# Attention and a top-1 mixture of experts on one core: the first expert tiles placed ahead of the last group's routing, the last expert's weights loaded in another order and place

## The reference

```python
x = x + attention(layernorm(x), ctx, ctx)     # per token: 16 x 16 scores over heads of width 16, causal over heads
xf = layernorm(x).reshape(4096, 256)
top1 = argmax(xf @ gate_w.T + gate_b)         # E = 8 experts
for e in range(8):                            # w1: 1024 x 256, w2: 256 x 1024
    y = relu(xf @ w1[e].T + b1[e]) @ w2[e].T + b2[e]
    out = out + where(top1 == e, y, 0)
x = x + out
```

## Time and profile before

| | us |
|---|---|
| runs | 484.26, 487.8, 488.61 (median 487.8) |
| profiled execution: its time | 486.96 |
| its span | 485.2 |
| PE busy | 397.5 (82%) |
| DVE busy | 348.3 (72%) |
| POOL busy | 206.3 (43%) |
| ACT busy | 179.6 (37%) |

### The profile page before, as it was taken

How to read it: one execution, slowest core, us unless ns; L and a number is a source line. 1 busy time by engine, 2 the same in 40 slices (tenths; PEclk the granted TensorE clock), 3 DMA queues, 4 the chain that set the end, 5 groups by cost and what they waited for, 6 DMA issues and landing times.

```text
span 485.2 us, 16314 instructions
## 1 busy us (share of the span) xinstructions
PE 397.5 (82%) x5967; PEld 337.0 (69%) x5967; DVE 348.3 (72%) x777; ACT 179.6 (37%) x317; POOL 206.3 (43%) x213
## 2 busy tenths in 40 slices
PE   0134868896887967987859999999999999999992
PEld 0024767796787866977847887777788878887871
DVE  7987879689965965777547886787666667666662
ACT  3333255552633332332323433334334333333420
POOL 8336375234574456623711342465332233232221
PEclk9999999999999755565559999999999999999998
DMA  8999668899786665676621423465333222222300
GB/s 287 415 296 237 139 149 238 213 269 261 172 212 141 157 134 125 161 162 124 218 61 33 79 83 123 132 192 179 70 71 76 77 64 64 70 63 67 85 24 0
DMA packets 105162, 69.39 MB, mean 143 GB/s; under 512 B 78077, under 2 KB 88190, under 8 KB 104576
## 3 DMA queue, kind: packets, MB, share of 16 engines
q1 hardware_dynamic: 75696, 56.67, 43.9%
q10 hardware_dynamic: 25984, 3.21, 4.8%
q0 software_dynamic: 3408, 8.46, 4.7%
HBM read 48.28 MB, written 12.57 MB: 125 GB/s over the span
## 4 chain that ended last, share of the span: by engine, by line
PE 58%; DMA 10%; POOL 7%; SPq 7%; issue 7%; DVE 6%; ACT 2%; ACTq 1%; POOLq 0%; DVEq 0%
PE s_ps L1216 22%; PE at_ps L1231 7%; DMA arena<-qv_hl 7%; PE pv_ps L1231 7%; SPq L298 7%; PE pv_ps L1130 5%; PE at_ps L1232 4%; PE pv_ps L1232 3%; PE s_ps L1098 3%; POOL sorted_rows L1037 2%; PE tr_ps L1143 2%; PE st_ps L1183 2%; DMA arena<-x 2%; POOL qv_hl L990 1%; PE lg_ps L1158 1%
## 5 line engine op out<-in xcount | busy, mean ns | idle before, releaser
L1216 PEld LDWEIGHTS s_ps<-arena 128*128 x1872 | 131.5, 99 | 44.3 <-issue 5.8
L1216 PE MATMUL s_ps<-arena 128*128 128x128 f16 x1872 | 156.8, 221 | 2.4 <-issue 2.3
L903 DVE SCALAR_TENSOR_TENSOR arena<-arena,s_ps 128x512 f32<-128x512 f32 x78 | 53.6, 687 | 43.6 <-PE s_ps L1216 43.5
L1063 POOL DMA_INDIRECT result<-arena x39 | 38.8, 995 | 79.1 <-DVE arena L927 76.6
L1098 PEld LDWEIGHTS s_ps<-k_hl,arena 128*128 128x128 f16 x1536 | 53.9, 118 | 26.1 <-DMA arena<-qv_hl 21.7
L1098 PE MATMUL s_ps<-k_hl,arena 128*128 128x16 f16 x1536 | 54.1, 181 | 19.6 <-DMA arena<-qv_hl 19.0
L1130 PE MATMUL pv_ps<-a_hl,arena 128*128 128x16 f16 x1536 | 53.9, 181 | 18.2 <-DMA arena<-qv_hl 14.0
L1130 PEld LDWEIGHTS pv_ps<-a_hl,arena 128*128 128x128 f16 x1536 | 52.7, 118 | 21.5 <-DMA arena<-qv_hl 19.0
L1056 POOL TENSOR_TENSOR arena<-arena 128x256 f32<-128x256 f32 x39 | 29.8, 764 | 75.5 <-DMA arena<-b 68.7
L1231 PE MATMUL at_ps<-arena,k_in 128*128 x160 | 60.3, 379 | 0.8 <-DVE k_hl L913 0.6
L1231 PE MATMUL pv_ps<-arena,x_in 128*128 x152 | 57.6, 379 | 0.2
(11 more groups left out here) (139 smaller groups left out, 616.4 us busy)
## 6 DMA issues: line engine op xcount, KB each, us to landing
arena<-w SPq DMA_DIRECT2D x28, 512.0 KB, 6.1
arena<-sorted_rows SPq DMA_DIRECT2D x39, 130.0 KB, 2.7
arena<-b SPq DMA_DIRECT2D x39, 128.0 KB, 3.7
arena<-qv_hl SPq DMA_DIRECT2D x70, 64.0 KB, 3.9
k_in<-k_t SPq DMA_DIRECT2D x16, 256.0 KB, 3.9
v_in<-v_t SPq DMA_DIRECT2D x16, 256.0 KB
arena<-x SPq DMA_DIRECT2D x4, 1024.0 KB, 12.2
o_sb<-x_r SPq DMA_DIRECT2D x16, 256.0 KB, 3.5
```

The costliest lines, as they stand in the source:

```text
L903: eng.scalar_tensor_tensor(out=h_in[:, c].rearrange("p (k t) -> p k t", t=P), in0=bias, scalar=W_SCALE, in1=h_ps[c][:].rearrange("p (k t) ...
L1063: eng.indirect_dma_start(out=out, out_offset=bass.IndirectOffsetOnAxis(ap=rows[:, r, :].bitcast(I32)[:, D + 2:D + 3], axis=0), in_=rows[:, ...
L1216: k = eng.matmul(o, weights_of(j, w + k_ * H + n * P, P), xt[:, j % 2, k_ * P:(k_ + 1) * P], start=k_ == 0 and w is HI_1 and xt is xt_hi, ...
```

## The change

The due times of the tiles start at 240.0 in place of 252.9. On PE the four pieces of transposes of group 3 and three of its four pieces of gate products are now due later, so that they fall among the matmuls of tiles 0 to 3; on ACT, DVE and POOL the group's copies and layer norm, the plan after group 2 and the last four scatters of group 2 are placed among tiles as well. The two w1 DMAs of expert 7 are due ahead of the last block's small value DMAs. Its w2 pieces 2 and 3 get buffers of their own, `v_in` and `a_sb`, which wait for the last values and the last transposed softmax, and semaphores `s_last`. The first up waits for 60 weight pieces; the first down, and the relus and splits of tile 1 on, wait for all 64.

```diff
--- before.py
+++ after.py
@@ -198,6 +198,7 @@
 
         s_xin = [sem(f"s_xin{n}") for n in range(2)]
         s_w = [sem(f"s_w{n}") for n in range(2)]
+        s_last = [sem(f"s_last{n}") for n in range(2)]
         s_own = [sem(f"s_own{n}") for n in range(2)]
         s_wide = [sem(f"s_wide{n}") for n in range(4)]
         s_xs = [sem(f"s_xs{n}") for n in range(NG)]
@@ -246,10 +247,10 @@
         UNIT = TILE / KH
 
         def tile_at(j):
-            return 252.9 + TILE * j
+            return 240.0 + TILE * j
 
         def fill_at(n):
-            return tile_at(7) + 4.5 + 4.0 * n
+            return 299.0 + 2.7 * n
 
         def halves(split, a):
             return split[:, :, :, :, a]
@@ -259,6 +260,8 @@
 
         def values_landed(i):
             return s_bd[i % 2], 128 * (i // 2 + 2)
+
+        last_home = v_in[:], a_sb[:]
 
         def chunk_of(n):
             e, c = n // PER_EXPERT, n % PER_EXPERT
@@ -266,6 +269,8 @@
                 src = of_expert(e + 1).bitcast(F32)[:, c * WC:(c + 1) * WC]
             elif c < 4:
                 src = of_expert(e).bitcast(F32)[:, KD * H + c * WC:KD * H + (c + 1) * WC]
+            elif e == E - 1 and c >= 6:
+                src = last_home[c - 6]
             else:
                 src = x_in[:, c % 2, :]
             if c < 4:
@@ -281,6 +286,8 @@
                 return s_wide[c // 2], 16 * (e + 1)
             if c < 4:
                 return s_own[e - WIDE], 32
+            if e == E - 1 and c >= 6:
+                return s_last[c - 6], 16
             return s_w[c % 2], 16 * (2 * (e - WIDE) + c // 2 - 1)
 
         x_v = x.rearrange("(g p b) d -> g p b d", p=P, b=G)
@@ -364,7 +371,7 @@
 
             def load_late():
                 for e in range(WIDE, E):
-                    yield (140.1, 234.2)[e - WIDE]
+                    yield (140.1, 225.6)[e - WIDE]
                     sp.wait_ge(s_w_lo, PER_EXPERT * WIDE)
                     if e == E - 1:
                         sp.wait_ge(s_qk, NC)
@@ -372,8 +379,12 @@
                         eng.dma_start(of_expert(e).bitcast(F32)[:, KD * H + c * 2 * WC:KD * H + (c + 1) * 2 * WC],
                                       w1[:, e, c * 2 * WC:(c + 1) * 2 * WC]).then_inc(s_own[e - WIDE], 16)
                     for c in range(4):
-                        yield (196.5, 189.5, 184.3, 186.2, 212.3, 239.5, 246.0, 248.4)[4 * (e - WIDE) + c]
+                        yield (196.5, 189.5, 184.3, 186.2, 237.5, 237.6, 237.7, 237.8)[4 * (e - WIDE) + c]
                         sp.wait_ge(s_q_lo, NC)
+                        if e == E - 1 and c >= 2:
+                            sp.wait_ge(*((s_v_lo, NC), (s_turned, NC))[c - 2])
+                            eng.dma_start(last_home[c - 2], w2[:, e, c * WC:(c + 1) * WC]).then_inc(s_last[c - 2], 16)
+                            continue
                         if c >= 2:
                             sp.wait_ge(s_w_lo, PER_EXPERT * e + c + 3)
                         elif e > WIDE:
@@ -513,7 +524,7 @@
                 for g in range(NG):
                     for n in range(4):
                         yield (95.1, 95.8, 97.7, 100.2, 153.3, 153.5, 146.3, 153.2, 199.4, 203.0, 208.5, 211.7,
-                               252.3, 254.2, 258.8, 258.6)[4 * g + n]
+                               255.5, 258.5, 261.5, 264.5)[4 * g + n]
                         act.wait_ge(s_o_t, 4 * g + n + 1)
                         act.wait_ge(s_scatter[0], 8 * G * g)
                         act.wait_ge(s_scatter[1], 8 * G * g)
@@ -538,7 +549,7 @@
                            31.9, 72.2, 71.5, 69.8, 68.5, 79.0, 78.9, 83.8, 65.6, 88.3, 92.5, 84.1, 89.8, 88.8, 95.7,
                            97.1, 81.9, 99.2, 99.9, 77.7, 104.9, 83.4, 109.0, 102.7, 101.1, 126.2, 124.0, 122.0,
                            117.7, 126.7, 134.1, 137.3, 135.2, 147.3, 148.0, 137.3, 150.1, 198.9, 171.9, 205.3, 193.6,
-                           232.6, 222.0, 242.5, 225.9, 230.8, 241.7, 244.9, 215.8)[n]
+                           228.1, 228.15, 228.2, 228.25, 241.6, 241.7, 241.8, 241.9)[n]
                     e, src, hi, _ = chunk_of(n)
                     act.wait_ge(*chunk_landed(n))
                     act.wait_ge(s_w_lo, PER_EXPERT * e if e < WIDE or n % PER_EXPERT < 4 else PER_EXPERT * e + 4)
@@ -565,6 +576,7 @@
                         yield tile_at(j) + 6.0 + 2.8 * c
                         act.wait_ge(s_h_in, 2 * j + c + 1)
                         act.wait_ge(s_down, j - 1)
+                        act.wait_ge(s_w_lo, CHUNKS if j else 0)
                         eng.activation(h_hi[j % 2][:, c * HALF:(c + 1) * HALF], h_in[:, c], ACT.Relu).then_inc(s_h_hi, 1)
 
             weave(spread_first_queries(), spread(), queries(), keys(), values(), turned_rows(), exponentials(), weights(), expert_inputs(), relus())
@@ -697,7 +709,7 @@
             def outputs():
                 for i in range(NC):
                     yield (67.1, 65.5, 96.0, 96.3, 122.4, 127.0, 140.4, 143.3, 170.7, 164.2, 178.2, 191.9, 222.0,
-                           216.4, 238.1, 246.2)[i]
+                           216.4, 238.1, 239.0)[i]
                     o = o_sb[:, i % CG * BLK:(i % CG + 1) * BLK, :]
                     dve.wait_ge(s_pv, i + 1)
                     dve.wait_ge(s_xr[i % CG], 16 * (i // CG + 1))
@@ -707,8 +719,8 @@
                 for g in range(NG):
                     for b in range(G):
                         yield (104.1, 107.9, 95.7, 107.2, 100.0, 96.1, 99.5, 98.7, 155.7, 158.9, 165.1, 167.1, 170.9,
-                               156.1, 154.0, 162.0, 213.8, 207.4, 221.1, 216.2, 202.9, 215.1, 209.4, 214.9, 258.1,
-                               261.6, 265.3, 246.4, 270.8, 264.0, 273.9, 275.5)[8 * g + b]
+                               156.1, 154.0, 162.0, 213.8, 207.4, 221.1, 216.2, 202.9, 215.1, 209.4, 214.9, 266.0,
+                               267.2, 268.4, 269.6, 270.8, 272.0, 273.2, 274.4)[8 * g + b]
                         dve.wait_ge(s_x1, 4 * g + 4)
                         dve.wait_ge(s_ln1, g)
                         eng.bn_stats(bn6[:, b, :], pay[:, b, 0:D]).then_inc(s_bn, 1)
@@ -802,75 +814,75 @@
 
                 for n, (_, count, g) in enumerate(STAGES):
                     so_far, last = PLAN * n, n == len(STAGES) - 1
-                    yield (195.0, 246.1, 303.7)[n]
+                    yield (195.0, 238.2, 303.7)[n]
                     dve.wait_ge(s_ranked, g + 1)
                     dve.wait_ge(s_table, TABLES)
                     dve.wait_ge(s_digit, 1)
...
                         eng.tensor_tensor(ready[:], ready[:], endless[:], ALU.max).then_inc(s_plan, 1)
                     else:
                         eng.tensor_scalar(ready[:], ready[:], 0.0, None, ALU.max).then_inc(s_plan, 1)
-                    yield (169.2, 248.8, 307.7)[n]
+                    yield (169.2, 250.0, 307.7)[n]
                     dve.wait_ge(s_plan, so_far + 4)
                     dve.wait_ge(s_slot, 4 * g + 4)
                     eng.tensor_tensor(by_slot[:, 0:E], lower[:], ready[:].unsqueeze(1).to_broadcast([1, E, E]),
                                       ALU.mult).then_inc(s_plan, 1)
-                    yield (189.5, 235.7, 304.5)[n]
...
+                    yield (192.0, 258.4, 333.1)[n]
                     eng.tensor_scalar(remains[:], below[:], -1.0, float(count), ALU.mult, ALU.add).then_inc(s_plan, 1)
-                    yield (162.3, 236.4, 300.5)[n]
+                    yield (162.3, 259.0, 300.5)[n]
                     dve.wait_ge(s_plan, so_far + 17)
                     eng.scalar_tensor_tensor(out=remains[:], in0=remains[:], scalar=0.0, in1=ready[:], op0=ALU.max,
                                              op1=ALU.min).then_inc(s_plan, 1)
-                    yield (186.0, 247.6, 287.1)[n]
+                    yield (186.0, 259.6, 287.1)[n]
                     dve.wait_ge(s_plan, so_far + 18)
                     eng.tensor_tensor(done[:], done[:], remains[:], ALU.add).then_inc(s_plan, 1)
 
@@ -881,7 +893,7 @@
                            49.8, 72.9, 84.7, 85.5, 85.5, 80.6, 70.8, 77.5, 88.5, 95.0, 96.7, 71.8, 86.8, 94.2, 98.1,
                            91.2, 96.1, 102.8, 93.4, 119.4, 117.0, 118.3, 119.9, 127.7, 116.4, 138.1, 123.7, 134.8,
                            133.7, 132.9, 142.3, 139.3, 141.9, 152.9, 143.0, 152.2, 142.2, 199.2, 190.3, 205.7, 187.3,
-                           247.5, 230.7, 229.1, 236.2, 238.8, 222.2, 230.4, 219.0)[n]
+                           238.3, 238.35, 238.4, 239.5, 242.5, 242.6, 242.7, 242.8)[n]
                     dve.wait_ge(s_w_hi, n + 1)
                     eng.scalar_tensor_tensor(out=lo, in0=src, scalar=W_SCALE, in1=hi, op0=ALU.mult,
                                              op1=ALU.subtract).then_inc(s_w_lo, 1)
@@ -910,6 +922,7 @@
                         cols = slice(c * HALF, (c + 1) * HALF)
                         yield tile_at(j) + 6.7 + 2.8 * c
                         dve.wait_ge(s_h_hi, 2 * j + c + 1)
```

(14 more changed lines are left out.)

32 lines of the change are left out of this document (16 added, 16 removed).

## The result

The changed kernel took 485.35 us (median of 20 runs, 479.88 to 489.61), the kernel before 488.2 in the 20 runs beside it (484.26 to 490.53). The ratio is 0.9924, with a 95% interval of 0.9899 to 0.9949: 3.7 us faster, where 10.4 were forecast. The ratio counts fast runs alone and so leaves out six of the changed kernel's twenty, those of 487.14 us and more, and none of before's; between the two medians above lie 2.85 us. The profiled execution took 484.82 us with a span of 483.1, 2.1 less than that of before.

A forecast was written before the change was run, and what follows sets the result against it. PE bounds the tiles from the first up, which waited for group 3's copies behind group 2's scatters. Gain 15.1 - 1.8 (gates) - 2.2 (transposes) - 0.7 (DVE) = 10.4 us: 477.4 against the median 487.8, range 473 to 484.

The forecast's parts named there:

- The start: First up at 236.9 against 252.14, 15.2 us earlier; tile 1's ups at 242.6 against 257.69, a gain of 15.1.
- the 1.0 us that I charged for it: Delay of the last values product by w1 ahead of the value DMAs on their queue; bounds nothing to 5.3 us.
- the first rival: Value DMAs wait behind w1's megabyte or issue slowly, delaying the last values product 4.3 us more; 481.7, chance 0.12.
- one for one beyond: w2 landing late behind the first up is free within 0.7 us of cover, then costs about its own lateness.
- Gate pieces: Two more gate pieces among the tiles on PE, each half of 1.76 us to all of it: 1.8, up to 3.5.
- DVE's crowding in tiles 1 to 5: Plan and statistics among the tiles exceed DVE's spare time and delay PE: nothing to 7.8 us, 0.7 taken.
- The second rival: DVE and ACT crowd in tiles 1 to 5: plan, statistics and copies cost 5.2 us more, 482.6; chance 0.13.
- The scatters of group 3 and the fills keep their distance in tiles: POOL and SP: fills still end one tile ahead of tile 17's fetch, as before; no cost charged.
- with no price: The plan's first four instructions, the fills and the third-group copies, all beside PE-bound tiles, were charged nothing.
- tile 17's wait for the fills: Example of a wait later than tile 5, uncovered by the early start, that would break the whole sum; no size given.
- the rival in which the start does not move: Rows or w2 land late, tile 0 waits, and 4.0 us of extra PE work stay: 485.4, chance 0.05.
- The clock: Rival: float32 pieces among the ups keep PE at half clock for some 2.6 tiles, 19 us more: 496.4, chance 0.07.

The follow-up runs named there:

- tiles_only: The changed kernel with w1 of expert 7 behind the value DMAs and w2's third and fourth pieces waiting for `x_in`, as before; ratio to before 1.0036.
- gates_less_after: The changed kernel without three of the last group's four gate pieces, so its experts are chosen by four heads alone; ratio to before 0.9882.
- phase_same: The changed kernel with group 3's choice, rank products, count and plan due 1.5 us earlier, fills and scatters unmoved; ratio to before 0.9874.

## Why the prediction was wrong

*The start: right in sum, in part by luck.* 15.1 us were forecast at the ups of tile 1, and 14.7 came. The first up gained 15.8 us where I had 15.2, since the values cost nothing, and the seam behind it cost 1.0 more than I had: two errors that nearly cancel. The gap from the last maximum to the last values product is 7.30 us in both kernels (231.79 - 224.49, and the earlier trace rows). The values do land later behind w1: the median of the five DMAs is 3.1 to 3.3 us in all eleven kernels with w1 ahead, and 2.2 in before and 2.3 in tiles_only. But about that much time was to spare, so the 1.0 us that I charged for it did not reach PE in the change, and the first rival fell: of the eleven, seven show 7.29 to 7.31 us, and four show 7.66 to 8.48, a delay of 0.4 to 1.2, where that rival wanted 5.3. In those four PE idles 0.57 to 1.40 us behind the DMA from `qv_hl`, the sign that I had named for it. The Trainium skill (DMA: Bandwidth & Descriptors, Queues, rings and completion order) has each DMA engine take a queue's descriptors in ring order; the later landings do not speak against it, but no run here shows it, and the price that I worked out for that case is in none of these traces. The step between tiles 0 and 1 took 6.67 us (238.31 to 244.98), 1.0 above my 5.7, which is the gate piece at 1.80 instead of 0.88.

*w2: not free, but covered by what I had not counted as cover.* Four issues went out without a wait for a buffer, as forecast. Issues and landings of the kernel after, from 231 to 239 (KB each, us to landing):

```profile
x_in<-w SPq DMA_DIRECT2D x2, 256.0 KB, 6.1
...
v_in<-w SPq DMA_DIRECT2D x1, 256.0 KB, 6.5
a_sb<-w SPq DMA_DIRECT2D x1, 256.0 KB, 6.9
```

They landed in 6.1 to 6.9 us and not in 3.9, and DVE's last split of w2 ended at 242.1, 3.8 us behind the first up, where I had 1.9 (238.8 - 236.9) with 0.7 of cover. By "one for one beyond" that is 1.2 us. PE lost none of it, because the gate piece at 243.18 stands in just that time; gates_less_after shows what appears without it, 1.79 us, 1.0 more than the 0.75 of before at that place.

*Gate pieces: a mis-sized term.* I named both ends, 0.88 and 1.76 us each, and took the lower, since the clock would be full. The upper holds, 1.81 at either clock. Two pieces behind the step took 3.6 us of PE and not 1.8; leaving them out gave back 2.5 to 2.9. The transposes took 1.85 in all, for 2.2.

*DVE's crowding in tiles 1 to 5: absent.* 257.69 to 278.06 in before, 20.37 us; 244.98 to 270.70 in after, 25.72. The difference of 5.35 is the two gate pieces and the four transposes (3.6 + 1.85 = 5.5): PE never waited for the plan or the statistics. The second rival fell in its place; tiles 1 to 5 had PE's own extra work to hide them.

*The step that failed: "The scatters of group 3 and the fills keep their distance in tiles" and the edits "with no price ... all beside PE-bound tiles".* I priced everything behind tile 5 at nothing, and 5.1 to 6.2 us were lost between tiles 8 and 17. It was wrong twice. I looked at the distance in tiles and not at the place within a tile: a choice of small instructions that stood ahead of a relu's low half in DVE's order moved to just ahead of the instruction that gates PE, and phase_same (20.4 to 18.6 us from tile 8 to 11 by a shift of 1.5 us) shows it. And an untouched due time is a moved one when its surroundings move: the choice, the count and so the fills of group 3 stayed where they were while tile 17 came 12.9 us earlier, two tiles less of distance, for which the new fills stand 2.7 apart instead of 4.0. Moving all of that routing up took 3.8 to 5.0 of the 5.1 to 6.2 us away; that the closer fills alone cost anything is not shown. I had named tile 17's wait for the fills as what would break the sum, without a price; in the change it was hidden behind the loss on DVE, and it decides as soon as that is mended.

*The sum again, with what was measured:* 14.7 - 3.6 - 1.8 + 0.0 (crowding) - 5.2 (5.1 from 8 to 17 and 0.1 from 5 to 8) = 4.1, the 243.2 - 239.1 of the table, and close to the 3.7 of the timed runs. From the forecast of 10.4: the late tiles took 5.2, the gate pieces 1.8, the start 0.4, while crowding and transposes gave 1.1 back. The measured 485.35 is the figure of the rival in which the start does not move (485.4), but by chance: the start did move, by 14.7 us.

*The clock: the rival fell.* Three gate pieces and four pieces of transposes in float32 among the ups of tiles 1 to 4 left it at 0.99 over tiles 1 to 5. The rule that PE-mode transposes do not count as busy in the same way as other matmuls (the Trainium skill, TensorE: Matmul & The Clock Gate, Part 4: PE-mode transpose) had spoken for that rival; here 0.61 us of them at a time stand between float16 matmuls, and no window shows an effect.

## What to carry to other kernels

When a stage is moved under an order of written due times, list every item whose time was not edited and whose neighbours moved, and ask for each where it now falls within a step and how far it is from its last user; moving by whole steps (here 11.4 us and not 12.9) should keep the first question shut, though no run moved the tiles so. A gain at the start of a stage that one engine bounds is only worth what the stage's later deadlines let through, so take each floor in turn, here DVE's order, then the fetches, then the fills. And an operation's time is halved by a doubled clock only if its own rows show it at both levels; where they don't, the range has to carry both ends and the choice needs a reason.

## What was not expected of the hardware

- The float32 weight loads of the gate products have the same pace at both clock levels: eight in 1.81 us at 1.2 GHz and in 1.82 at 2.4 GHz. Those of the float32 transposes do not: four took 0.72 us at 1.2 GHz (before, 233.94) and 0.53 at 2.4 GHz (after, 254.05), and the transposes themselves went from 1.12 to 0.61. Why the two differ was not tried.
- Five small value DMAs issued behind 1 MB of weights on the same queue landed about 1 us later (median 3.1 to 3.3 us for 2.2), and cost their user nothing in seven profiles of eleven and at most 1.2 us in the others: 7.30 us from maximum to product with and without the weights. Why those four differ was not tried.
- 3.00 us without a matmul, at a granted clock of 1.00, were followed by 6 us at 0.50 (tiles_only, 242 to 248), in which six matmuls of the ups took 0.84 us for 0.50.
- 256 KB took 6.1 to 6.9 us to land beside the fetches and scatters of 231 to 239, where the median before was 3.9. The DMA share was 1.03 from 236 to 240 there and 0.42 in before, which had scatters in that time as well.
- The attention stage ended anywhere within 4.5 us (220.35 to 224.80) in kernels that share its instructions, more than what most of these edits are worth. Only counting from its end made two profiles comparable.
